# Softmax denominators moved from TensorE to VectorE, and a new order of GpSimd's and VectorE's work in each attention step

## What is computed

```
def attn(latents, context):                 # latents = layernorm(x)
    lat, ctx = layernorm(latents, ln_l_w, ln_l_b), layernorm(context, ln_c_w, ln_c_b)
    q, (k, v) = lat @ Wq, split(ctx @ Wkv)  # by head
    s = clip(einsum('bhnd,bhsd->bhns', q, k) * 64 ** -0.5, -11, 11)
    return einsum('bhns,bhsd->bhnd', softmax(s), v).merge_heads() @ Wo + bo
x = x + attn(layernorm(x), ctx_1024)
x = x + ffn(layernorm(x))                   # int8 fake-quantised silu(gate) * up, then down
```

## Time and profile before

| | |
|---|---|
| median of 3 runs | 1309.81 us (1308.99 to 1311.67) |
| the profiled execution | span 1307.3 us from its first to its last instruction; the launch around it isn't in the page |
| TensorE busy | 1273.7 us, 97% of the span |
| VectorE busy | 1147.7 us, 88% |
| ScalarE busy | 805.3 us, 62% |
| GpSimd busy | 302.5 us, 23% |
| granted TensorE clock | 1.000 of full over the span |

### The profile page before, as it was taken

The page is one execution under the profiler, slowest core; times in us unless marked ns, Lnnn a source line. Parts: engine busy times, 40 slices in busy tenths (PEclk is TensorE's granted clock), DMA queues, the critical chain, the costliest instruction groups (busy, mean ns, idle before and its releaser), DMA issues.

```text
span 1307.3 us, 20769 instructions
## 1 busy us (share of the span) xinstructions
PE 1273.7 (97%) x7756; PEld 605.4 (46%) x7800; DVE 1147.7 (88%) x2086; ACT 805.3 (62%) x1211; POOL 302.5 (23%) x230
## 2 busy tenths in 40 slices
PE   6999999999999999999999999999999999989998
PEld 4644444544445445445445444444444444434443
DVE  7777988898998889899888848799999999889998
ACT  6589577567557757755775762233333333399993
POOL 3105242244134224413422420000000000013223
PEclk9999999999999999999999999999999999999999
DMA  7276057247146355462562392196667642389997
GB/s 298 78 238 186 22 150 223 68 129 202 65 142 181 106 163 120 125 206 57 159 227 73 106 240 87 45 306 229 198 259 249 217 173 85 113 306 420 421 420 305
DMA packets 182437, 241.76 MB, mean 185 GB/s; under 512 B 122032, under 2 KB 141248, under 8 KB 169920
## 3 DMA queue, kind: packets, MB, share of 16 engines
q1 hardware_dynamic: 182336, 240.43, 55.6%
HBM read 120.86 MB, written 90.57 MB: 162 GB/s over the span
## 4 chain that ended last, share of the span: by engine, by line
PE 65%; DVE 13%; ACT 12%; DMA 4%; issue 3%; SPq 1%; POOL 1%; DVEq 0%; ACTq 0%
PE pg L1584 10%; PE pu L1590 10%; PE po L77 7%; PE po L79 7%; PE po L78 7%; PE ring L79 6%; PE ring L77 6%; PE ring L78 6%; ACT hb L1448 6%; DMA out_dram<-xqT 1%; ACT E L452 1%; DMA x<-in_x_dram 1%; PE ring L1039 1%; PE ring L1066 1%; ACT E L446 1%
## 5 line engine op out<-in xcount | busy, mean ns | idle before, releaser
L1426 ACT ACTIVATE sg<-pg,gate_scale 128x512 f32<-128x512 f32 x176 | 121.0, 687 | 184.0 <-PE pg L1584 184.0
L77 PE MATMUL ring<-yT,M 128*128 128x512 f16 x512 | 194.1, 379 | 0.0
L79 PE MATMUL ring<-yT,M 128*128 128x512 f16 x512 | 194.0, 379 | 0.0
L78 PE MATMUL ring<-yT,M 128*128 128x512 f16 x512 | 194.0, 379 | 0.0
L77 PE MATMUL po<-VW,p 128*128 128x512 f16 x480 | 182.2, 380 | 1.7 <-DVE p L660 1.7
L79 PE MATMUL po<-VW,p 128*128 128x512 f16 x480 | 181.9, 379 | 0.0
L78 PE MATMUL po<-VW,p 128*128 128x512 f16 x480 | 181.9, 379 | 0.0
L1584 PE MATMUL pg<-xqT,w 128*128 128x512 bf16 x690 | 178.8, 379 | 2.2 <-ACT xqT L1437 0.8
L1590 PE MATMUL pu<-xqT,w 128*128 128x512 bf16 x689 | 178.6, 379 | 0.8
L395 POOL TENSOR_TENSOR esum<-esum,E 128x512 f32<-128x512 f32 x96 | 130.5, 1359 | 83.8 <-ACT E L456 83.8
L467 ACT ACTIVATE p<-E 128x512 f16<-128x512 f32 x120 | 74.9, 625 | 121.6 <-DVE E L656 119.6
(11 more groups left out here) (246 smaller groups left out, 2060.0 us busy)
## 6 DMA issues: line engine op xcount, KB each, us to landing
hidden<-hb SPq DMA_DIRECT2D x11, 2816.0 KB, 9.9
xa<-x_rows_d SPq DMA_DIRECT2D x28, 1024.0 KB, 5.6
hb<-hidden SPq DMA_DIRECT2D x22, 1024.0 KB, 16.4
x<-in_x_dram SPq DMA_DIRECT2D x16, 1024.0 KB, 5.7
value_fold<-E SPq DMA_DIRECT2D x64, 256.0 KB, 2.5
VW<-value_fold SPq DMA_DIRECT2D x16, 1024.0 KB, 6.0
x_rows_d<-x SPq DMA_DIRECT2D x16, 1024.0 KB, 4.6
out_dram<-xa SPq DMA_DIRECT2D x11, 1024.0 KB, 13.3
```

The costliest lines, as they stand in the source:

```text
L77: nc.tensor.matmul(out, a_hi, b_hi, start=first, stop=False)
L78: nc.tensor.matmul(out, a_hi, b_lo, start=False, stop=False)
L79: return nc.tensor.matmul(out, a_lo, b_hi, start=False, stop=last)
L1426: nc.scalar.activation(sg[:, n % 4], pg[n % 4][:], ACT.Silu, scale=gate_scale[:, n % FT:n % FT + 1]).then_inc(silus, 1)
```

## The change

On TensorE `denominators` and `turn_back` go (and with them the constants `head_rows` and `head_cols` of the opening). VectorE makes the denominators itself in `invert`: it transposes `esum` in 32x32 blocks, so that a row's eight partial sums of a head lie side by side, sums them (`tensor_reduce`), inverts, and transposes a broadcast of the inverses back into the PSUM tile `pd`. The factor `PROB_GAIN`, that was in `head_cols`, moves into `divide`, which becomes a `scalar_tensor_tensor`.

The order changes too. GpSimd's additions of step s, for s from 2 to 14, start only when the last `low` of group s-1 and the last `low_y` of group s+1 are done, and the four biases follow them; in step 1 the biases follow the additions; step 0 is as before. `rescale(s)` is run in step s for its own group instead of in step s-1. VectorE's statistics, aggregates and rstd of group s+1 move from the outputs part of step s-1 into the score part of step s (t = 0 to 2), `norm_rows` to t = 3, 3, 5, 6 and `low_y` to t = 4, 5, 7, 7; `unit_range` moves from behind `invert` to ahead of `take(s-1, 0)`.

```diff
     def row_beside(s, t):
-        return t // 2 if t % 2 == 1 and s + 1 < NG and (s > 1 or t >= 5) else None
+        if s + 1 == NG:
+            return None
+        return {5: 2, 7: 3}.get(t) if s == 1 else {3: 0, 4: 1, 6: 2, 7: 3}.get(t)
+
+    NORM_BESIDE = ((), (), (), (0, 1), (), (2,), (3,), ())
+    LOW_BESIDE = ((), (), (), (), (0,), (1,), (), (2, 3))
...
         def add_up(g, t):
             pool.wait_ge(exps, 8 * g + t + 1)
             if t == 1:
-                wait(pool, dens, g)
+                wait(pool, sums_turned, g)
...
         for s in range(NG):
             more = s + 1 < NG
+            if s > 1 and more:
+                pool.wait_ge(prob_lo, 8 * s)
+                pool.wait_ge(y_lo, 4 * (s + 1) + TT)
             for t in range(1, KT):
                 add_up(s, t)
-                if more and t >= 4:
+                if s == 0 and t >= 4:
                     bias(s + 1, t - 4)
+            if s > 0 and more:
+                for t in range(TT):
+                    bias(s + 1, t)
...
-                if s == 1 and t == 1:
-                    rescale(1)
-                if more and t == 1:
-                    rescale(s + 1)
+                if t == 1:
+                    rescale(s)
...
         def invert(g):
+            dve.wait_ge(sums, 7 * g + 7)
+            nc.vector.transpose(esumT[:].rearrange("p n s -> p (n s)"), esum[:]).then_inc(sums_turned, 1)
+            dve.wait_ge(sums_turned, g + 1)
+            nc.vector.tensor_reduce(dsum[:], esumT[:], AX.X, ALU.add).then_inc(dens, 1)
             dve.wait_ge(dens, g + 1)
-            nc.vector.reciprocal(rtok[:].rearrange("p t h -> p (t h)"), pd[:, 0:TT * H]).then_inc(rdens, 1)
-            dve.wait_ge(rdens, 2 * g + 1)
-            nc.vector.tensor_copy(rexp[:], rtok[:].rearrange("p t (h a) -> p t h a", a=1).broadcast_to((P, TT, H, KS))).then_inc(rdens, 1)
+            nc.vector.reciprocal(rsum[:], dsum[:]).then_inc(rdens, 1)
+            dve.wait_ge(rdens, g + 1)
+            wait(dve, prob, 8 * g)
+            nc.vector.transpose(pd[:].rearrange("p (n s) -> p n s", s=KS),
+                                rsum[:].rearrange("p (n a) -> p n a", a=1).broadcast_to((P, GT // KS, KS))).then_inc(rden_turned, 1)
...
-            nc.vector.tensor_tensor(E[:, g % 2, t], E[:, g % 2, t], pd[:], ALU.mult).then_inc(prob, 1)
+            nc.vector.scalar_tensor_tensor(E[:, g % 2, t], E[:, g % 2, t], PROB_GAIN, pd[:], ALU.mult, ALU.mult).then_inc(prob, 1)
...
-                if more and t % 2 == 0 and (s > 1 or t >= 4):
-                    norm_rows(s + 1, t // 2)
-                if row_beside(s, t) is not None:
-                    low_y(s + 1, row_beside(s, t))
+                if s == 1:
+                    if t in (4, 6):
+                        norm_rows(s + 1, t // 2)
+                    if t in (5, 7):
+                        low_y(s + 1, t // 2)
+                    continue
+                if not more:
+                    continue
+                if t < 2:
+                    norm_stats(s + 1, (2 * t, 2 * t + 1))
+                if t == 2:
+                    norm_aggregates(s + 1)
+                    norm_rstd(s + 1, s + 1)
+                for k in LOW_BESIDE[t]:
+                    low_y(s + 1, k)
+                for k in NORM_BESIDE[t]:
+                    norm_rows(s + 1, k)
...
+            if s <= UNITS:
+                unit_range(s - 1)
             take(s - 1, 0)
             if more:
                 for u in FOLD_AFTER[0]:
                     fold(s, u)
             invert(s)
-            if s <= UNITS:
-                unit_range(s - 1)
-            if ahead:
-                norm_stats(s + 2)
-                norm_aggregates(s + 2)
             if more:
                 take(s - 1, 1)
                 for u in FOLD_AFTER[1]:
                     fold(s, u)
-                if ahead:
-                    norm_rstd(s + 2, s + 2)
                 round_unit(s - 1)
...
-        def denominators(g):
-            pe.wait_ge(sums, 7 * g + 7)
-            wait(pe, prob, 8 * g)
-            for t in range(TT):
-                ins = nc.tensor.matmul(pd[:, t * H:(t + 1) * H], esum[:, t * P:(t + 1) * P], keep.head_cols[:], start=True, stop=True)
-            ins.then_inc(dens, 1)
-
-        def turn_back(g):
-            pe.wait_ge(rdens, 2 * g + 2)
-            for t in range(TT):
-                ins = nc.tensor.transpose(pd[:, t * P:(t + 1) * P], rexp[:, t].rearrange("p h s -> p (h s)"), keep.ident32[:])
-            ins.then_inc(rden_turned, 1)
```

More of the change, by code:

```diff
@@ L112, in attention @@
     esum = sb("esum", [P, GT], fp32)
-    rtok = sb("rtok", [P, TT, H], fp32)
-    rexp = sb("rexp", [P, TT, H, KS], fp32)
+    esumT = sb("esum_by_token", [P, GT // KS, KS], fp32)
+    dsum = sb("den_by_token", [P, GT // KS], fp32)
+    rsum = sb("rden_by_token", [P, GT // KS], fp32)
     stage = E[:, 1].rearrange("p t n -> p (t n)").bitcast(fp16).rearrange("p (k a q n) -> p k a q n", k=4, a=2, q=2)
@@ L181, in attention @@
     scores, capped, floored, exps, sums = sem("scores"), sem("capped"), sem("floored"), sem("exps"), sem("sums")
-    dens, rdens, rden_turned = sem("dens"), sem("rdens"), sem("rden_turned")
+    sums_turned, dens, rdens, rden_turned = sem("sums_turned"), sem("dens"), sem("rdens"), sem("rden_turned")
     prob, prob_hi, prob_lo = sem("prob"), sem("prob_hi"), sem("prob_lo")
@@ L375, in on_gpsimd @@
                                    base=0, pattern=[[-1, P]], channel_multiplier=1))
[L376 to L380, removed]
         nc.gpsimd.memset(magic[:, 0:1], MAGIC).then_inc(magic_set, 1)
@@ L597, in on_vector, with norm_stats @@
         ln = Counter(dve, ln_step)
-        def norm_stats(g):
+        def norm_stats(g, tiles=range(TT)):
             dve.wait_ge(x_loaded[g % 4], 16 * (g // 4) + 16)
             wait(dve, ln_step, ln.n)
-            for t in range(TT):
+            for t in tiles:
                 nc.vector.bn_stats(st[:, t, :], x[:, g % 4, t, :]).then_inc(ln_step, 1)
-            ln.n += TT
+            ln.n += len(tiles)
         def norm_aggregates(g):
@@ L769, in vectors_seen @@
             nc.vector.tensor_scalar(row_reach, keep.ident32[0:4 * DC, 0:4 * DC], amax[0:4 * DC, 0:1], None, ALU.mult).then_inc(spread_in, 1)
-            dve.wait_ge(const_turned, 2)
-            do(nc.vector.tensor_scalar(keep.head_cols[:], misc[:, 4 * DC:4 * DC + H], 1.0 / PROB_GAIN, None, ALU.mult))
+            dve.wait_ge(const_turned, 1)
             do(nc.vector.tensor_copy(cols[:].rearrange("p k c -> p (k c)"), misc[:, 0:4 * DC]))
@@ L902, in on_vector @@
             more = s + 1 < NG
-            ahead = s + 2 < NG
             for t in range(KT):
@@ L1077, in fold, with output @@
                 fold_values(values_folded_in(s), u // 2)
-        def output(g, t, between):
+        def output(g, t):
             if t == 0:
@@ L1090, in output @@
                                      k == 0, k == KT - 1)
-                if k == 1 and t in (1, 2):
-                    between(t - 1)
             ins.then_inc(outs, 1)
@@ L1136, in product @@
             if n == 0:
-                pe.wait_ge(made, 5 + 2 * DC)
+                pe.wait_ge(made, 2 + 2 * DC)
                 pe.wait_ge(w_lo[1], DC)
@@ L1169, in turn_q @@
             ins.then_inc(q_turned, 1)
-        pe.wait_ge(made, 5)
-        nc.tensor.transpose(misc[:, 4 * DC:4 * DC + H], keep.head_rows[:], keep.ident32[0:H, 0:H]).then_inc(const_turned, 1)
+        pe.wait_ge(made, 2)
         pe.wait_ge(ld_vec, 64)
@@ L1219, in on_tensor @@
                     fold_values(0, t // 2)
[L1220 to L1229, removed]
             for t in range(TT):
                 if s > 0:
-                    output(s - 1, t, between)
+                    output(s - 1, t)
                     for u in FOLD_AFTER[t]:
@@ L1237, in on_tensor @@
         for t in range(TT):
-            output(NG - 1, t, lambda k: None)
+            output(NG - 1, t)
     return on_sync, on_gpsimd, on_scalar, on_vector, on_tensor
@@ L1646, in program @@
         keep.ident32 = sb("ident32", [P, P], fp32)
-        keep.head_cols = sb("head_cols", [P, H], fp32)
-        keep.head_rows = sb("head_rows", [H, P], fp32)
         keep.own_row = sb("own_row", [P, KS], fp32)
```

## The result

The changed kernel takes 1312.27 us (median of 20 runs, 1309.91 to 1313.63); beside it, on the same chips, the kernel before takes 1309.94. The ratio is 1.0016, 95% interval 1.0009 to 1.0022: within the 0.2% taken here for no change, if anything above it. Forecast were 1298.5; what came is the case "between the two", to which 0.08 was given.

A forecast was written before the change was run, and what follows sets the result against it. TensorE was taken as the bound, at 45.82 us a step. Removing 1.24 us in 14 steps gives 17.4, less 6.1 lost to the ring is 11.3: from the median 1309.8 to 1298.5 us, range 1290 to 1313.

The forecast's parts named there:

- between the two: Rival: L from 45.8 to 46.2 us, no measurable change, 1307 to 1312 us; chance 0.08.
- (b): GpSimd's seven additions after the last `low_y`, 1.23 us from start to start: 8.65 us.
- the ring: Chain once around each step without TensorE, through VectorE's divides, ScalarE's copies, GpSimd's additions, `invert`, takes and folds: 45.15 us.
- the formula: Kernel time in us: 1292.4 + 13 (L - 44.58) - 1.3, and 1292.4 when L is below 44.7.
- (a): From the start of `divide(s-1, 2)` through ScalarE's chain to the end of the last `low_y`: 22.8 us.
- (d): VectorE's queue behind `invert`: takes, folds, `round_unit` and the next step's first divides and low, 11.1 us.
- (c): `invert` on VectorE: two transposes taken at 0.68 us each, reduction 0.69, reciprocal 0.55, with gaps 2.65 us.
- longer than the old period: Rival: GpSimd's sum and VectorE's inversion, one behind the other, make the kernel slower, from L = 46.0 us on; chance 0.20.
- L: Length in us of the ring in each step, forecast at 45.15.
- TensorE stays the bound: Rival: transposes at the copy's rate make L 44.65 us, so 1292.4 us, or 1290 with step 1's gain; chance 0.22.
- The y transposes: Rival: DMA transposes of y land late, each us over 1.7 entering the ring; 1300 to 1310 us, chance 0.03.
- I count step 1 at nothing: In step 1 TensorE already waited 2.9 us for `low`, so removing its pieces gains nothing, from -2 to +2 us.

The follow-up runs named there:

- the version with one wait less: The changed kernel without GpSimd's wait for the last `low_y`, its additions released by the last `low` alone: 1292.41 us, ratio 0.9866.
- The run with two sums: The changed kernel with GpSimd's seven additions in two partial sums used by turns, the seventh adding the two: 1300.78 us, ratio 0.9937.
- The runs in the old order: The kernel before without TensorE's two pieces: with denominators on VectorE, 1327.79 us; with nothing in their place and divides by a constant, 1304.76 us.
- the denominators alone: The kernel before with `invert` making the denominators on VectorE and TensorE's pieces gone, all else in the old order: 1327.79 us, ratio 1.0139.

## Why the prediction was wrong

**The step that failed** is term (b) of the ring: "Seven additions, 1.23 us from start to start". It measures 9.9 us instead of 8.65. The rest of the argument held: what TensorE loses (44.58 a step in the version with one wait less), the ring and its four pieces, the formula, and the place of TensorE's new waits. The mechanism was right and a term was mis-sized. The 1.26 us alone would make 16 us in 13 steps and 1315; that the miss is only 13.8 is partly luck, since (a) and (d) together came 0.46 us shorter than forecast, while a mean step is 0.14 longer than the one in the table. The run with two sums took this one term back to 8.98 and landed at 1300.8. A slip besides: the terms given for (c) add up to 2.72, not to 2.65; 2.69 was measured.

**The prediction had the warning in hand.** It named the spacing of the additions (above 1.3) among the things that would make it wrong, and priced 1.45 in the rival "longer than the old period". Against that rival it held that "every term but the transposes has a row". What it had not done is ask whether the row it took, an addition followed by an independent bias, was of the kind that would stand in the ring. In the old order a chain of dependent additions never stood back to back, since each waited for its tile, so before's trace does not show this distance.

**The rivals.** "Between the two" is what happened, with L = 46.18 in its 45.8 to 46.2. "TensorE stays the bound" failed for (b) and not for (c), where it had looked for it. The y transposes were not seen late.

**Right.** The two transposes at 0.71 and 0.73 us against 0.68 taken; the estimate worked out from the Trainium skill (VectorE: DVE Perf Modes, The three transpose paths) was 0.71 each, and agrees. The small scaling in `unit_range`, which by the Trainium skill (SBUF — State Buffer, on port sharing) could have waited up to 1.2 us, took 0.27 instead of 0.17. In steps 2 to 14 `low` takes 0.68 to 0.69 us, without the 1.76.

**Right for a poor reason.** Of the old order the prediction said "Before, GpSimd added while the tiles came, and nothing waited", and read VectorE's idle time as room. The runs in the old order put a ring of about 45.5 us there, 0.3 below the bound, and in three steps of before's own trace that ring, not TensorE, is the chain that ended last. VectorE's idle time was no room. The forecast did not use this sentence in its sum, but the expectation for the denominators alone did, and missed by over 30 us. The new order did more than make room for the wait in (b): without it the change loses 18 us.

**Step 1.** "I count step 1 at nothing" came within 0.2 us at its second fold group, in part by luck: the wait of 2.2 us for `turn_back(0)`, which the prediction did not name, went as well, and a clock at half for 6 us, which it did not foresee, took the gain back.

**Where the gain went.** TensorE's 17.4 us are there to be had. Of the two waits that hold GpSimd back, the one for the last `low_y` costs them all, as it puts the sum, 9.9 us, behind the last `low_y` of the score part. Without it the kernel takes 1292.4 us, 1.4% below before.

## What to carry to other kernels

When work is taken off the engine that bounds a loop, add up the ring of hand-overs that goes once around through the other engines, before and after: idle time on an engine that stands in such a ring is not room. Look for it in the trace before: where the chain that ended last leaves the bounding engine for whole steps, a second ring is about as long. Take each term from a row with the same dependence, not only the same shape: here 0.18 us between a dependent and an independent instruction, six times a step in 13 steps, is 14 us, more than the whole forecast gain. When an order is made to keep two engines apart, set what the contention costs (here 1.8 us a step) against the start that it delays (5.9 us).

## What the runs showed of the hardware

- GpSimd's 128x512 fp32 addition starts 1.23 us after an independent one and 1.41 us after one whose result it reads, through a semaphore.
- VectorE's 32x32 block transpose of 128x512 fp32 takes 0.71 us, and 0.73 from a broadcast source into PSUM.
- VectorE's two-input `low_y` takes 0.69 us with GpSimd idle, 0.94 and 1.47 beside its additions; an addition of GpSimd's takes 1.27 alone and 1.50 beside VectorE.
- After the change TensorE's granted clock fell to 0.50 after waits of 2.5 and 2.4 us, 2.7 us apart, in step 1, and was back at 1.00 in the window from 143 us on. Before, it stayed at 1.00 through one wait of 2.2 us at 119 us and two of 1.3 and 1.4 at 137 and 138 us.
